# Packed key columns in a windowed attention: own and cross blocks in separate banks, and a stacked remainder in the down projection

## The reference

```python
def _layer(x, wqkv, qs, ksc, wo, lg, lb, w1, b1, w2, b2):
    h = shift_token(x)
    q, k, v = split_heads(h @ wqkv)              # 8 heads of 64
    q, k = rotary_xpos(l2norm(q) * qs, l2norm(k) * ksc)
    x = x + merge(local_attention(q, k, v)) @ wo # window 128: own and previous window of keys
    h = layernorm(shift_token(x)) * lg + lb
    a, g = split(h @ w1 + b1)                    # hidden 682 each
    return x + (a * gelu(g)) @ w2 + b2
# in local_attention: mask = (i < j) | (i > j + 128) | (j == -1)
```

## Time and profile before

| | |
|---|---|
| median of the runs | 2045.06 us |
| profiled execution: time / span | 2045.3 / 2043.5 us |
| PE busy | 1900.0 us (93%) |
| DVE busy | 1327.4 us (65%) |
| ACT busy | 1386.6 us (68%) |
| POOL busy | 960.7 us (47%) |
| granted TensorE clock, mean | 0.989 |

### The profile page before, as it was taken

The page is one execution under the profiler, slowest core; times in us unless marked ns, Lnnn a source line. Parts: engine busy times, 40 slices in busy tenths (PEclk is TensorE's granted clock), DMA queues, the critical chain, the costliest instruction groups (busy, mean ns, idle before and its releaser), DMA issues.

```text
span 2043.5 us, 42506 instructions
## 1 busy us (share of the span) xinstructions
PE 1900.0 (93%) x15184; PEld 1576.0 (77%) x15184; DVE 1327.4 (65%) x4125; ACT 1386.6 (68%) x3869; POOL 960.7 (47%) x1311
## 2 busy tenths in 40 slices
PE   6999999999999789999999999999999999999998
PEld 4778777777777668778788787787887878878777
DVE  4544543444443467777768777787777776877775
ACT  5886877778678465775766757657567575675764
POOL 2432442434243463644726537457265473663732
PEclk9999999999999889999999999999999999999999
DMA  3322231313225411010110101304101011010010
GB/s 127 109 80 66 75 118 44 97 60 88 92 66 162 151 39 32 19 43 12 45 45 12 42 22 37 104 6 161 55 6 52 22 45 55 22 42 27 31 33 27
DMA packets 122261, 121.10 MB, mean 59 GB/s; under 512 B 27188, under 2 KB 100804, under 8 KB 122052
## 3 DMA queue, kind: packets, MB, share of 16 engines
q1 hardware_dynamic: 118884, 112.10, 17.2%
q10 hardware_dynamic: 3168, 6.29, 0.9%
HBM read 72.72 MB, written 37.25 MB: 54 GB/s over the span
## 4 chain that ended last, share of the span: by engine, by line
PE 32%; DVE 20%; ACT 9%; issue 3%; POOL 3%; DVEq 0%; ACTq 0%; SPq 0%; POOLq 0%
PE f_bank L1383 11%; PE f_scores L1523 5%; PE f_scores L1461 4%; ACT f_prob L1598 4%; DVE f_u L1751 4%; PE f_bank L1509 4%; PE f_bank L1469 4%; DVE f_gu L1748 2%; PE f_o_bank L1484 2%; ACT f_u L1618 2%; PE f_bank L1434 2%; DVE y_tok L1734 2%; DVE y_tok L1740 1%; POOL f_prob L1336 1%; DVE f_rstd L1727 1%
## 5 line engine op out<-in xcount | busy, mean ns | idle before, releaser
L1336 POOL TENSOR_SCALAR f_prob<-f_prob,f_row_inv 128x256 f32<-128x256 f32 x512 | 263.0, 532 | 331.2 <-DVE f_row_inv L1694 331.1
L587 POOL TENSOR_SCALAR a_prob<-a_prob,a_row_inv,a_gate 128x128 f32<-128x128 f32 x512 | 224.4, 455 | 407.8 <-DVE a_row_inv L927 407.8
L1383 PE MATMUL f_bank<-weights,f_actT 128*128 128x512 f32 x1152 | 301.8, 406 | 1.6 <-DVE f_actT L1637 1.6
L1509 PE MATMUL f_bank<-f_hT,f_w 128*128 128x256 f32 x2112 | 276.2, 286 | 7.6 <-DVE f_gu L1748 7.6
L1509 PEld LDWEIGHTS f_bank<-f_hT,f_w 128*128 128x128 f32 x2112 | 261.9, 190 | 14.2 <-DVE f_gu L1748 10.7
L1598 ACT ACTIVATE f_prob<-f_scores,f_neg_max 128x256 f32<-128x256 f32 x512 | 235.8, 487 | 32.6 <-DVE f_neg_max L1686 31.6
L1383 PEld LDWEIGHTS f_bank<-weights,f_actT 128*128 128x128 f32 x1152 | 208.4, 191 | 50.3 <-ACT f_probT L1545 5.4
L1686 DVE CUSTOM_DVE_ANT_0 f_scores<-f_scores,f_mask 128x256 f32<-128x256 f32 x512 | 199.8, 456 | 14.8 <-PE f_scores L1461 14.7
L1312 POOL TENSOR_TENSOR f_norm<-f_norm,f_minus_half 128x16 f32<-128x16 f32 x64 | 198.6, 3104 | 21.5 <-DVE f_norm L1646 18.9
L1618 ACT ACTIVATE f_u<-f_gu 128x256 fp32r<-128x256 f32 x192 | 80.2, 418 | 179.4 <-DVE f_gu L1748 179.4
L819 ACT ACTIVATE a_prob<-a_scores,a_neg_max 128x128 f32<-128x128 f32 x512 | 179.5, 390 | 27.8 <-DVE a_neg_max L918 26.5
(11 more groups left out here) (129 smaller groups left out, 3834.5 us busy)
## 6 DMA issues: line engine op xcount, KB each, us to landing
split_weights<-a_hi_lo SPq DMA_DIRECT2D x16, 512.0 KB, 2.8
x_next<-states SPq DMA_DIRECT2D x32, 256.0 KB, 3.2
tables<-scaled_tables SPq DMA_DIRECT2D x16, 512.0 KB, 6.2
f_x<-states SPq DMA_DIRECT2D x16, 512.0 KB, 5.5
split_weights<-a_hi_lo SPq DMA_DIRECT2D x12, 682.0 KB, 4.2
weights<-split_weights ACTq DMA_DIRECT2D x6, 1024.0 KB, 9.7
f_w<-split_weights SPq DMA_DIRECT2D x4, 1280.0 KB, 10.8
a_x_tok<-in_x SPq DMA_DIRECT2D x8, 512.0 KB, 4.4
```

Source lines behind the costliest of these rows:

```text
L587: last = nc.gpsimd.tensor_scalar(part, part, row_inv[:, a % 2, head, t:t + 1], gate[:, half, t, h:h + 1], ALU.mult, ALU.mult)
L1336: last = nc.gpsimd.tensor_scalar(part, part, row_inv[:, a % 2, head, t:t + 1], 1.0, ALU.mult, ALU.mult)
L1383: last = nc.tensor.matmul(out, lhs(c, a), rhs(c, b), start=(i == 0), stop=(i == len(order) - 1))
L1509: mm = nc.tensor.matmul(out[:, which * PART:(which + 1) * PART], w1[:, wp, c, col:col + P], hT[:, hp, c, columns_of(a // FH)], start=(i == ...
```

## The change

- `scores`: for each tile the queries are cut into two halves of 64, and their 192 keys are put into 192 columns. 128 "own" columns hold whole tiles: the previous tile's keys for the first half of the queries, the own tile's for the second. 64 "cross" columns hold the rest: half of the own tile for the first half, half of the previous one for the second. In the first tile of a unit the own columns stand first, in the second the cross columns, so that the cross columns of both lie side by side. One matmul becomes three (192, 128 and 64 columns) with 64 stationary columns. The masked minimum, exp and scaling run over 192 columns and not 256.
- `transpose`: six blocks and not eight. Four own blocks of both heads fill one bank, two cross blocks another. ACT empties the first with one copy of 512 columns and the second with two copies of 64 partitions x 256 columns. `probT` holds zeros in the places that no copy writes.
- `values`: the own tile's two halves, the neighbour's and two products with `v_crossed`, a copy of v whose halves of 64 keys are brought together by four DMAs for each half (`cross_values`, a new step on SP). Up to five matmuls a head (256, 64, 64, 64, 64 columns), before up to three (256, 128, 128).
- `down`, sixth block: the low part of u is written at partitions 64 to 105 of the high part's tile, and the high part of w2 is loaded there a second time; two passes with 106 rows take the place of three with 42.
- To make room, `square` holds one of q and k, no longer both: the square of k waits for the sum of q's squares.
- POOL clears `v_crossed`, `probT`, w2's last block and part of u at the start of the stage.

```diff
-        mask = sb("mask", [P, 2, 2 * P])
+        mask = sb("mask", [P, 3, KEYS])
+        PACKED = (((FIRST, slice(0, KEYS), 0), (SECOND, slice(P, 2 * P), 0), (SECOND, SECOND, P)),
+                  ((SECOND, slice(BLOCK, 2 * P), 0), (FIRST, slice(0, P), BLOCK), (FIRST, slice(P, KEYS), 0)))
-        square = sb("square", [P, 2, CHUNK])
+        square = sb("square", [P, CHUNK])
...
-                            for head in (0, 1):
-                                rows = slice(DH * head, DH * (head + 1))
-                                mm = nc.tensor.matmul(scores[a % 2][head][:, t, :], q[rows, pair, col:col + P],
-                                                      kT[rows, pair, col:col + 2 * P], start=True, stop=True)
+                            for queries, keys, place in PACKED[t]:
+                                for head in (0, 1):
+                                    rows = slice(DH * head, DH * (head + 1))
+                                    mm = nc.tensor.matmul(scores[a % 2][head][queries, t, place:place + keys.stop - keys.start],
+                                                          q[rows, pair, col:col + P][:, queries],
+                                                          kT[rows, pair, col:col + 2 * P][:, keys], start=True, stop=True)
...
+                        packed = [prob[:, a % 2, head].rearrange("p t k -> p (t k)") for head in (0, 1)]
+                        out = take_bank(it, filled.number(it, (kind, a), 0))
                         for head in (0, 1):
-                            out = take_bank(it, filled.number(it, (kind, a), head))
                             pe.wait_ge(normalized.sem, normalized.past(it, ("weigh", a), head))
-                            for j in range(4):
...
+                            for t in (0, 1):
+                                place, source = (2 * head + t) * P, 2 * P * t
+                                last = nc.tensor.transpose(out[:, place:place + P], packed[head][:, source:source + P], ident[:])
+                        last.then_inc(filled.sem, 1)
+                        out = take_bank(it, filled.number(it, (kind, a), 1))
+                        for head in (0, 1):
+                            last = nc.tensor.transpose(out[:, head * P:(head + 1) * P], packed[head][:, P:2 * P], ident[:])
+                        last.then_inc(filled.sem, 1)
...
-                        order = [(tile, P, 3 * P, 0, 2 * P), (tile + 1, 3 * P, 4 * P, P, 2 * P)]
+                        order = [(values_of(half, tile), 2, 0, 2 * P), (values_of(half, tile + 1), 7, P + BLOCK, BLOCK), (crossed, 1, P, BLOCK)]
                         if half or tile:
-                            order = [(tile - 1, 0, P, 0, P)] + order
+                            order += [(crossed, 6, BLOCK, BLOCK), (values_of(half, tile - 1), 0, 0, BLOCK)]
...
+                        order = [(m, up, wp) for up, wp in PASSES] if j < FH - 1 else [(STACKED.stop, HI, HI), (STACKED.stop, HI, LO)]
...
+                    if kind == "transpose" and i == 0:
+                        nc.scalar.activation(place[0], bank[n % 3][:].rearrange("p (k b n) -> p k b n", k=4, b=2), ACT.Copy).then_inc(copied.sem, 1)
+                    elif kind == "transpose":
+                        cross = bank[n % 3][:, 0:2 * P].rearrange("p (k n) -> p k n", k=4)
+                        nc.scalar.activation(place[0], cross[FIRST], ACT.Copy)
+                        nc.scalar.activation(place[1], cross[SECOND], ACT.Copy).then_inc(copied.sem, 1)
...
-                    if ("project_qk", a - 1) in emptied.firsts(it):
-                        act.wait_ge(emptied.sem, emptied.past(it, ("project_qk", a - 1), which))
+                    if which == KEY:
+                        act.wait_ge(emptied.sem, emptied.past(it, ("project_qk", a), QUERY))
+                    elif ("project_qk", a - 1) in emptied.firsts(it):
+                        act.wait_ge(emptied.sem, emptied.past(it, ("project_qk", a - 1), KEY))
...
+            pool.memset(v_crossed[FIRST, 0], 0.0)
+            pool.memset(probT[:], 0.0)
...
+            pool.memset(w2[:, :, FH - 1, :].bitcast(F32), 0.0)
+            pool.memset(u[:, 1::2, HI, :].bitcast(F32), 0.0).then_inc(zeroed, 1)
```

99 lines of the change are left out of this document (62 added, 37 removed).

## The result

The changed kernel takes 2028.86 us in the median of five runs (2027.12 to 2031.62), the kernel before 2044.9 us beside it. One run of the kernel before, 2335.24 us, was in a slower state and does not count in the ratio, which is 0.9933 with a 95% interval of 0.9922 to 0.9943: 16 us are gained by the medians, 12 to 16 by the ratio, where 38 were forecast. The profiled execution has a span of 2027.0 us.

What follows compares the result with a forecast made beforehand. PE was taken to lead at 95% busy, with POOL also full in the middle. Gains of 0.6, 1.3 and 0.6, 2.5 us a half over 15.5 halves, made -39, preamble +1: 2045.3 - 38 = 2007 us, range 1978 to 2034.

Steps and rivals of the forecast that it cites:

- PE's savings: On PE: scores -31 us, transposes -27, values +6, down's sixth block -16; sum -68 us.
- Rival 1: Whole kernel: PE's saving of 68 us arrives whole, 1977 us; chance 13%.
- Rival 4: Scores: unequal pieces run one after another, +50 us in place of -31, total 2058 us; chance 4%.
- Rival 5: Matmuls: each has its own price however narrow, 34 ns; 24 take 0.82 us; given no chance beside the first case.
- my case: Whole kernel: the main forecast, 2.5 us gained a half, 2007 us, own range 1986 to 2023; chance 54%.
- The new wait: Square of k waits for DVE's sum: 0.5 us at a half's first project_qk, 0.6 at the third on ACT alone.
- middle: Half's stretch from POOL's first norm to its first layer-norm power: POOL loses idle time, 1.3 us gained a half.
- front: Half's stretch from PE's transposes of x to POOL's first norm: that norm starts 0.6 us early.
- Rival 2: Third and first project_qk: the single square buffer binds, 24 us back, 2031 us; chance 19%.
- over 60 us: Sign: ACT waiting for DVE's f_norm before a square, under 20 us in total expected; over 60 would be rival 2.
- rest: Half's stretch from POOL's layer-norm power to the next start: block 5 gives 0.2, block 11 0.4, 0.6 us a half.
- Rival 3: PE's clock falls in its new idle time, once a half costing 24 us, 2031 us; chance 8%.

Runs made afterwards that it cites:

- experiment 6: The changed kernel with POOL's power for q's norms alone, 8 columns and not 16: 2021.85 us, ratio 0.9892.
- packed kernel: The changed attention without the square buffer's wait, the same kernel as in-bank: 2006.2 us, ratio 0.9814.
- in-bank: The changed kernel without square buffer and new wait: ACT writes squares into the bank they come from, DVE sums them there; 2006.2 us, ratio 0.9814.
- experiment 13: in-bank with ACT's second cross copy to probT left out: 1991.64 us, ratio 0.9761.
- experiment 14: The kernel before with only the down projection's sixth block stacked, two passes of 106 rows for three of 42: 2038.97 us, ratio 0.9977.
- experiments 15 and 9: Both on in-bank: 15 does each transpose of x twice in the layers, 2004.54 us; 9 does the second tile's scores matmuls twice, 2011.54 us.
- experiment 3: The changed kernel with only the third project_qk's squares of each half written into their banks, without the wait: 2009.72 us, ratio 0.9845.
- POOL runs: POOL's power on 8 columns, not 16: changed kernel 2021.85 us, in-bank 2000.14 us, kernel before 2031.03 us.
- experiment 7: in-bank with POOL's power for q's norms alone, 8 columns and not 16: 2000.14 us, ratio 0.9782.

## Why the forecast was too high

**PE's savings.** Scores 0.82 us and transposes 0.63 are as forecast. A unit's values take 1.05 us by themselves (1159.74 to 1160.79) where they took 1.02, and 1.95 for two in a row where 1.89 stood: +0.03 a unit, the forecast had +0.05. The Trainium skill (TensorE: Matmul & The Clock Gate, "Wait — 56ns, not 53.3ns?") has the sequencer spend about 62 ns on a matmul when hardware decode is off; if that held here, the 24 rows of a unit would take 1.49 us, and they take 0.82, 34 ns each. PE's busy time fell by 38.3 us and not 65. Some 13 us of the difference may be clock: the mean grant went from 0.989 to 0.982, 0.7% of 1862. The rest I cannot place. PE's idle time rose by 22 us, near the 25 of the prediction, but not where it said: PE's waits before transposes for POOL hardly changed (16.6 to 19.9 us); the new ones are before project_qk, for DVE's sum (11.1) and ACT's copy (7.8), and before scores, for exp (16.3 to 24.6).

**Rivals 1, 4 and 5.** Rival 1 is out: even without the wait 38 of PE's 68 us arrive. Rival 4 is out by the scores' 0.82 us. Rival 5 forecast the same 0.82, so these rows cannot tell it from my case.

**DVE, ACT and POOL.** The mask gave 66 ns, as forecast, exp 64 where I had 49. The three copies to probT take 1.27 us from the first's start to the next step's (1155.62 to 1156.89), against 0.95 for two before (1160.95 to 1161.90): +0.3 a unit where I took 0.1. POOL's scaling fell by 60 ns, from 532 to 472, where I had 0 to 30.

```profile
1160.95 1.11 ACT L1545 ACTIVATE f_probT<-f_bank 128x512 f32<-128x512 f32 x2
```

**The new wait is the step that failed.** I had worked out that ACT would stand 1.4 us at the third square, and then took 0.6, "on ACT alone", because DVE would come earlier. My sum took nothing off the middle for it; it took only 0.5 us a half off the front, for the first square. But the third wait grew to 1.56 us. Counted from POOL's first norm, DVE's sum of q starts 9.46 us on, 0.3 earlier than before (9.74), as it still stands behind rope_sum 0, 2.4 us in a row; ACT is ready for the square of k at 8.62, 0.4 earlier (9.06 before). The second half of the step, that a delay on ACT leaves the middle alone because the middle is POOL's, is wrong too: POOL has 0.75 and 1.36 us of idle time in the middle, and its relief does not bring the wait's cost back (experiment 6). The wait takes 1.13 us a half in the middle (29.70 to 28.57) and 0.32 in the front (14.03 to 13.71) in halves without a fall of the clock. Over 15.5 halves that is 22.5 us, and by the medians 22.7, against the 9 that I had booked (0.5 a half and 1 in the preamble).

**Rival 2** had the place and, with 2031, nearly the time (2028.9), at a chance of 19%. That its 24 us agree with the 22.7 is partly luck: they were to come on top of the 9 already booked, 33 in all. And my test for it, "over 60 us" of waiting, was wrong: 24.4 us of waiting cost 22.7, since nearly every microsecond arrived.

**Front, middle and rest.** Without the wait the packed kernel gives 0.43, 1.17 and 0.87 a half, 2.5. That in-bank's 2006 is also the 2007 on record is partly luck. My 0.6, 1.3 and 0.6 had already taken 0.5 off the front for the wait, so without one I had 1.1 there, and it gave 0.43. This is a second term that was too large, by 10 us in all, and some 4 of these the rest gave back. Why the front gave so little is open. The three copies on ACT are a candidate: experiment 13, with one of them less, shortens most fronts from 13.71 to 13.11. The rest was under-counted: the next half's first two scores units run before its start mark, so their saving lands there beside that of the stacked blocks (0.64 in experiment 14). So of the 22 us that are missing some 14 are the wait's beyond what was booked, and the others are the front's and the middle's, less what the rest gave more.

**Who paces.** "PE leads, POOL is full in the middle" was right of the kernel before: in its middle 1.0 of 1.3 us put on PE arrives, and POOL's relief gives 12 us. Once both are relieved neither does so any longer (0.1 of 1.0 us, and 6 us), so summing PE's terms further was of little use: put back on the packed kernel they cost about a sixth of their size (12 of 69 us by the medians).

**Rival 3, the clock.** After the change the granted clock falls at the start of six of the 14 halves, behind PE's idle moments of 0.93, 0.44 and 0.30 us there; before it fell at none of these starts. The idle moments are not new, though: at the same place the kernel before has 1.02, 0.45 and 0.82 us, without a fall. Its PE there:

```profile
1144.39 0.63 PE L1469 MATMUL f_bank<-ident,f_prob 128*128 128x128 f32 x4 [0.45 <-POOL f_prob L1336]
1145.84 0.66 PE L1469 MATMUL f_bank<-ident,f_prob 128*128 128x128 f32 x4 [0.82 <-DVE f_actT L1637]
```

So why the clock falls there after the change is not shown; that more work of PE removes the falls is: experiments 15 and 9 have none at these starts, and all their runs had a mean grant of 0.989 to 0.991. Windows of the changed kernel:

```profile
974.20:977.60 3.40, 2.56 (x34) 1.47 (x30) 1.80 (x6) 2.98 (x11) 3.23 (x8) 0.75 0.81 211
977.60:981.00 3.40, 3.40 (x32) 3.10 (x29) 2.34 (x15) 3.33 (x13) 0.23 (x1) 0.50 0.66 248
981.00:984.40 3.40, 3.40 (x16) 2.44 (x17) 0.46 (x2) 3.10 (x12) 2.41 (x7) 0.74 0.00 0
```

This, the longest, makes its front 14.57 us and its middle 30.26, against 14.03 and 29.70; the other five cost 0.2 to 0.4 each. That is 2.6 us of the missing 22, and not 24. Runs of one kernel bear on the whole: experiment 3's took 2008 us at a mean grant of 0.989 and 2015.3 at 0.979. By that, the step from the kernel before (0.989 in its profile) to the changed one (0.981 to 0.985 in its runs) is worth 3 to 6 us, an estimate, and part of it may stand in the 22.7 above, as in-bank's runs had 0.979 to 0.986.

## What to carry to other kernels

When an edit folds two buffers into one, the price of the new wait is read from what stands ahead of the releasing instruction on its engine, after every engine has been moved by the rest of the edit; if the waiting engine gains time and the releasing one does not, the wait grows. Count a wait in full unless a run shows slack behind it. And once the leading engine is relieved, stop adding up its terms: repeat a piece of its work in the new kernel and see how much of it arrives, with the piece's size read from that run's trace and its place in the stretches, not from the total alone.

## What the runs showed of the hardware

**POOL's scaling depends on what DVE reads.** In the changed kernel four scalings of 192 columns take 1.62 us at 1164.64, while DVE works mostly on the scores banks in PSUM, 2.28 at 1158.72 and 2.60 at 1174.62, where DVE has instructions with two operands in SBUF (L1711, and L1700 with its twin L1701):

```profile
1175.33 0.68 DVE L1700 TENSOR_TENSOR f_sin_part<-f_qk_tok,tables 128x512 f32<-128x512 f32 x1
```

The Trainium skill says that POOL and a DVE instruction with two SBUF inputs exclude each other for its whole length (SBUF — State Buffer, "SBUF: two separate sides"). For the scalings the trace agrees in part: the extra 0.66 and 0.98 us stay under the overlaps, 0.79 us with L1711 and 1.29 with L1700 and L1701. The power does not show it: at 1161.75 it has L1700 and L1701 inside it (1162.97 to 1164.23) and takes 2.91 us. In the POOL runs part of the relief was lost in the scalings: with the power on 8 columns in-bank's went from 476 to 522 ns, 24 us back of the 81 that the power gave. That they then met such instructions more often is not shown.

**The power's price is not in proportion to its columns.** 16 columns take 3.00 us (in-bank), 8 take 1.74 (experiment 7), and 2 take 0.75 (the power for the layer norm at 1179.66):

```profile
L1337 POOL TENSOR_TENSOR f_norm<-f_norm,f_minus_half 128x16 f32<-128x16 f32 x64 | 192.0, 3000 | 24.5 <-DVE f_norm L1687 21.3
```
```profile
L1337 POOL TENSOR_TENSOR f_norm<-f_norm,f_minus_half 128x8 f32<-128x8 f32 x64 | 111.2, 1738 | 37.6 <-DVE f_norm L1687 36.7
```

**The clock.** At in-bank's worst fall (granted 0.50, the lower level of 1.2 GHz) the first project_qk took 4.45 us, against 3.37 in the half before. That half and the next, which has such a fall too, took 81.9 and 81.4 us, their neighbours 80.1 and 80.5.

```profile
1135.18 4.45 PE L1408 MATMUL f_bank<-weights,f_actT 128*128 128x512 f32 x12
```
